# Half of the mask matmuls of the attention scores go: the second head of a pair is added onto the bank of the first, with the keys beside their negative

## The reference

```python
q = X @ Wq.T + bq                      # 32 heads of 16
k = encoder_output @ Wk.T + bk         # 8 groups of 16
v = encoder_output @ Wv.T + bv
scores = einsum('bgrqd,bgkd->bgrqk', q, k) / sqrt(16)
scores = where(causal_mask[None, None, None, :, :], -inf, scores)
scores = where(padding_mask[:, None, None, None, :], -inf, scores)
w = softmax(scores, axis=-1)
out = einsum('bgrqk,bgkd->bgrqd', w, v)
```

## Time and profile before

| | |
|---|---|
| time, median of 3 runs | 1948.77 us (1947.23 to 1953.24) |
| the profiled execution | 1954.19 us, span 1952.4 us |
| busy in the span | TensorE 86%, VectorE 55%, POOL 42%, ScalarE 38% |
| phase A | to about 625 us of the span |
| mean granted TensorE clock | 0.95 of full |

### The profile page before, as it was taken

One profiled execution on the slowest core, in us unless ns is written; L12 is line 12 of the kernel. 1 busy time (PEld: TensorE's weight loads), 2 busy tenths in 40 slices (PEclk: granted clock), 3 DMA queues, 4 the chain that ended last, 5 costly groups with the idle time before them and its releaser, 6 DMA issues. The chain is left out here.

```text
span 1952.4 us, 28974 instructions
## 1 busy us (share of the span) xinstructions
PE 1677.2 (86%) x10458; PEld 864.4 (44%) x10458; DVE 1077.9 (55%) x2244; ACT 736.4 (38%) x1326; POOL 828.0 (42%) x853
## 2 busy tenths in 40 slices
PE   5798888887875588888699996999999999888897
PEld 3455545444442243443266563444444444333343
DVE  6678777768663677776155664237755333211126
ACT  2468667666665454444122321221111111122221
POOL 1668656656455344444234532523534342011134
PEclk8999999999987799999799998999999999999999
DMA  5622123123022344443335442734654554366645
GB/s 144 157 66 80 47 55 82 44 55 77 17 68 63 59 97 101 93 93 77 60 69 130 97 87 56 161 88 104 146 112 105 114 124 98 71 151 155 153 132 181
DMA packets 423499, 188.82 MB, mean 97 GB/s; under 512 B 364792, under 2 KB 387576, under 8 KB 423360
## 3 DMA queue, kind: packets, MB, share of 16 engines
q1 hardware_dynamic: 417680, 168.36, 37.9%
q0 software_dynamic: 5680, 18.62, 3.4%
HBM read 77.82 MB, written 22.81 MB: 52 GB/s over the span
## 5 line engine op out<-in xcount | busy, mean ns | idle before, releaser
L894 POOL TENSOR_TENSOR a_pl<-a_prob,a_ph 128x512 f16<-128x512 f32 x256 | 298.5, 1180 | 206.1 <-ACT a_prob L810 204.7
L137 PE MATMUL bank<-XTh,d_whs 128*128 128x512 f16 x512 | 194.7, 380 | 0.9 <-ACT e_y L2256 0.7
L139 PE MATMUL bank<-XTh,d_wls 128*128 128x512 f16 x512 | 194.5, 380 | 0.0
L138 PE MATMUL bank<-XTl,d_whs 128*128 128x512 f16 x512 | 194.5, 380 | 0.0
L809 ACT ACTIVATE a_ph<-bank 128x512 f16<-128x512 f32 x256 | 154.3, 603 | 100.7 <-PE bank L612 77.0
L992 DVE TENSOR_REDUCE a_mx<-bank 128x2 f32<-128x512 f32 x256 | 165.7, 684 | 32.9 <-PE bank L598 29.7
L2094 POOL CAST d_cut<-d_raw 128x512 f16<-128x512 f32 x90 | 58.0, 645 | 234.3 <-DMA d_raw<-in_L_ffn_sw 152.7
L810 ACT ACTIVATE a_prob<-bank 128x512 f32<-128x512 f32 x256 | 155.2, 606 | 0.0
L2014 DVE TENSOR_TENSOR d_hid<-d_hid,bank 128x512 f32<-128x512 f32 x64 | 43.9, 686 | 181.6 <-PE bank L139 179.7
L610 PE MATMUL bank<-a_maddT,ident 128*128 128x512 f16 x256 | 103.4, 404 | 30.1 <-ACT a_prob L810 28.2
L1227 PE MATMUL bank<-b_wfc,b_xTh 128*128 128x512 f16 x256 | 99.5, 389 | 32.3 <-DMA b_xTl<-f_cut 25.9
(11 more groups left out here) (325 smaller groups left out, 4081.5 us busy)
## 6 DMA issues: line engine op xcount, KB each, us to landing
d_raw<-in_L_ffn_w SPq DMA_DIRECT2D x48, 256.0 KB, 3.0
d_raw<-in_L_ffn_sw SPq DMA_DIRECT2D x42, 256.0 KB, 3.1
made<-e_y SPq DMA_DIRECT2D x39, 256.0 KB
a_stage<-in_L_ffn_w_fc SPq DMA_DIRECT2D x32, 256.0 KB, 2.8
a_stage<-in_L_ffn_w_proj SPq DMA_DIRECT2D x32, 256.0 KB, 3.1
a_fbuf<-in_ctx SPq DMA_DIRECT2D x16, 256.0 KB, 3.7
rows<-f_cut SPq DMA_DIRECT2D x16, 256.0 KB, 2.4
out_x<-X SPq DMA_DIRECT2D x16, 256.0 KB
```

Of the source, the lines that this page charges most:

```text
L137: nc.tensor.matmul(out_ap, lhi, rhi, start=first, stop=False)
L138: nc.tensor.matmul(out_ap, lhi, rlo, start=False, stop=False)
L139: return nc.tensor.matmul(out_ap, llo, rhi, start=False, stop=last_one)
L894: nc.gpsimd.tensor_tensor(pl[:, n % NP, :], prob[:, n % 2, :], ph[:, n % NP, :], ALU.subtract).then_inc(ev["L"], 1)
```

## The change

A group in `ks` gets three slots: negated keys `kn`, keys `kp`, and zero. The pair (kp, 0) serves the first half and the pair (kn, kp) the second. The first half's matmul adds the upper head's scores to the mask, as before. The second half's matmul goes into the same bank without a new mask, after the first was read: it takes the upper head's scores (with its padding and maximum) away and adds the lower head's. The mask matmul is issued for `half == 0` alone. In the second pass n and n + 2 are the two halves and share a bank already; in the first pass the new `which` orders m so that m and m + 2 do. ScalarE's second copy of the high part is scaled by -1; VectorE makes the low parts of `kp` and `kn` in two subtractions of 128 x 128 where there was one of 128 x 256; `pad` holds the padding with both signs.

```diff
-    ks = sb("a_ks", [P, 2, G0, 4, STK], F16)
-    kd = ks[:, :, :, 0:4:3, :]
+    ks = sb("a_ks", [P, 2, G0, 3, STK], F16)
+    kn, kp = ks[:, :, :, 0, :], ks[:, :, :, 1, :]
...
+    def which(m):
+
+        u = m % 16
+        return m // 16, 2 * (u // 4) + u % 2, u // 2 % 2
...
# turn_k
-                        c = ks[:, tt, 4 * h + j // 2, 2 * (j % 2):2 * (j % 2) + 2, :].rearrange("p d c -> p (d c)")
+                        c = ks[:, tt, 4 * h + j // 2, 1 - j % 2:3 - j % 2, :].rearrange("p d c -> p (d c)")
...
# scores, and the same for tt, g, half in maxima
-                tt, g, half = m // 16, m // 2 % G0, m % 2
+                tt, g, half = which(m)
...
-                nc.tensor.matmul(bk[:, :].rearrange("p (r k) -> p r k", r=2), ident16[:, :],
-                                 madd[:, tt, :].unsqueeze(1).broadcast_to([P, 2, S]), start=True, stop=False)
+                if half == 0:
+                    nc.tensor.matmul(bk[:, :].rearrange("p (r k) -> p r k", r=2), ident16[:, :],
+                                     madd[:, tt, :].unsqueeze(1).broadcast_to([P, 2, S]), start=True, stop=True)
                 for r in range(2):
                     last = nc.tensor.matmul(bk[:, r * S:(r + 1) * S], qT[:, par, 2 * g + r, tt * P:(tt + 1) * P],
-                                            kT[:, par, 2 * g + half, :], start=False, stop=(r == 1))
+                                            kT[:, par, 2 * g + half, :], start=False, stop=True,
+                                            skip_group_check=True)
...
# turned_scores
-                nc.tensor.matmul(bk[:, :].rearrange("p (r k) -> p r k", r=2), ident16[:, :],
-                                 maddT[:, kc, :].unsqueeze(1).broadcast_to([P, 2, S]), start=True, stop=False)
+                if half == 0:
+                    nc.tensor.matmul(bk[:, :].rearrange("p (r k) -> p r k", r=2), ident16[:, :],
+                                     maddT[:, kc, :].unsqueeze(1).broadcast_to([P, 2, S]), start=True, stop=True)
...
# high_kv (ScalarE)
-                nc.scalar.activation(kd[:, tt, :, :, 0:HD0], k4, ACT.Copy)
-                nc.scalar.activation(kd[:, tt, :, :, 2 * HD0:3 * HD0], k4, ACT.Copy).then_inc(ev[f"hk{tt}"], 1)
+                nc.scalar.activation(p4, k4, ACT.Copy)
+                nc.scalar.activation(n4, k4, ACT.Copy, scale=-1.0).then_inc(ev[f"hk{tt}"], 1)
...
# low_kv (VectorE)
-                nc.vector.tensor_tensor(kd[:, tt, :, :, HD0:2 * HD0], k4, kd[:, tt, :, :, 0:HD0],
+                k3 = k32[:, tt, :].rearrange("p (g c) -> p g c", g=G0)
+                nc.vector.tensor_tensor(kn[:, tt, :, HD0:2 * HD0], kp[:, tt, :, 0:HD0], k3, ALU.subtract)
+                nc.vector.tensor_tensor(kp[:, tt, :, HD0:2 * HD0], k3, kp[:, tt, :, 0:HD0],
                                         ALU.subtract).then_inc(ev[f"lk{tt}"], 1)
```

More of the change, by code:

```diff
@@ L344, in phase_a @@
     maddT = sb("a_maddT", [P, 2, S], F16)
-    pad = sb("a_pad", [P, 2, B])
+    pad = sb("a_pad", [P, 2, B, 2])
     q32 = sb("a_q32", [P, D])
@@ L609, in turned_scores @@
                 wait("E", b, n + 1, NS)
-                nc.tensor.matmul(bk[:, :].rearrange("p (r k) -> p r k", r=2), ident16[:, :],
-                                 maddT[:, kc, :].unsqueeze(1).broadcast_to([P, 2, S]), start=True, stop=False)
+                if half == 0:
+                    nc.tensor.matmul(bk[:, :].rearrange("p (r k) -> p r k", r=2), ident16[:, :],
+                                     maddT[:, kc, :].unsqueeze(1).broadcast_to([P, 2, S]), start=True, stop=True)
                 nc.tensor.matmul(bk[:, :], kT[:, par, 2 * g + half, kc * P:(kc + 1) * P],
                                  qT[:, par, 2 * g:2 * g + 2, :].rearrange("p r q -> p (r q)"),
-                                 start=False, stop=True).then_inc(ev["ST"], 1)
+                                 start=False, stop=True, skip_group_check=True).then_inc(ev["ST"], 1)
             def times_v(b, par, n):
@@ L747, in high_kv @@
                 k4 = k32[:, tt, :].rearrange("p (g c) -> p g c", g=G0).unsqueeze(2).broadcast_to([P, G0, 2, HD0])
+                p4, n4 = (t[:, tt, :, 0:3 * HD0].rearrange("p g (r c) -> p g r c", r=3)[:, :, 0:3:2, :] for t in (kp, kn))
                 nc.scalar.activation(vv[:, par, tt, :, 0:HD0], v32[:, tt, :].rearrange("p (g c) -> p g c", g=G0),
                                      ACT.Copy).then_inc(ev[f"hv{tt}"], 1)
-                nc.scalar.activation(kd[:, tt, :, :, 0:HD0], k4, ACT.Copy)
-                nc.scalar.activation(kd[:, tt, :, :, 2 * HD0:3 * HD0], k4, ACT.Copy).then_inc(ev[f"hk{tt}"], 1)
+                nc.scalar.activation(p4, k4, ACT.Copy)
+                nc.scalar.activation(n4, k4, ACT.Copy, scale=-1.0).then_inc(ev[f"hk{tt}"], 1)
             def take_second(b, par, tt):
@@ L960, in bias_kv @@
                 wait(f"KV{tt}", b)
-                nc.vector.tensor_copy(kd[:, tt, :, :, ONE],
-                                      pad[:, tt, b:b + 1].unsqueeze(1).broadcast_to([P, G0, 2]))
+                nc.vector.tensor_copy(ks[:, tt, :, 0:2, ONE], pad[:, tt, b:b + 1, :].broadcast_to([P, G0, 2]))
                 nc.vector.tensor_tensor(v32[:, tt, :], bank[BM + 1][:, KV:2 * KV], bkv[:, KV:2 * KV], ALU.add)
@@ L974, in low_kv @@
                 wait(f"hk{tt}", b)
-                k4 = k32[:, tt, :].rearrange("p (g c) -> p g c", g=G0).unsqueeze(2).broadcast_to([P, G0, 2, HD0])
-                nc.vector.tensor_tensor(kd[:, tt, :, :, HD0:2 * HD0], k4, kd[:, tt, :, :, 0:HD0],
+                k3 = k32[:, tt, :].rearrange("p (g c) -> p g c", g=G0)
+                nc.vector.tensor_tensor(kn[:, tt, :, HD0:2 * HD0], kp[:, tt, :, 0:HD0], k3, ALU.subtract)
+                nc.vector.tensor_tensor(kp[:, tt, :, HD0:2 * HD0], k3, kp[:, tt, :, 0:HD0],
                                         ALU.subtract).then_inc(ev[f"lk{tt}"], 1)
@@ L1018, in _ @@
             nc.vector.memset(qs[:, :, :, ONE:ONE + 1], 1.0)
-            nc.vector.memset(kd[:, :, :, :, NEG:NEG + 1], 1.0)
+            nc.vector.memset(kp[:, :, :, NEG:NEG + 1], 1.0)
+            nc.vector.memset(kn[:, :, :, NEG:NEG + 1], -1.0)
             nc.vector.memset(vv[:, :, :, :, HD0:HD0 + 1], 1.0)
@@ L1039, in _ @@
             dve.wait_ge(k_tr, 1)
-            klink(nc.vector.tensor_copy(pad[:, :, :], bank[0][:, 0:2 * B].rearrange("p (t b) -> p t b", t=2)))
+            nc.vector.tensor_scalar(pad[:, :, :, 0], bank[0][:, 0:2 * B].rearrange("p (t b) -> p t b", t=2), -1.0, None,
+                                    ALU.mult)
+            klink(nc.vector.tensor_copy(pad[:, :, :, 1], bank[0][:, 0:2 * B].rearrange("p (t b) -> p t b", t=2)))
             dve.wait_ge(k_tr, 2)
```

## The result

The change makes the kernel slower: 1964.75 us median of five executions (1961.9 to 1968.88), where the kernel before took 1951.83 in five of its own, a ratio of 1.0064 with a 95% interval of [1.0046, 1.0082]. The forecast was 1936.7 us. The time lies above the range of 1923 to 1954 us, and the kernel became slower where faster was forecast.

The account below looks back on a forecast made before the run. TensorE and VectorE were taken as almost equally full in the scoring parts, with VectorE the bound beyond its waits. Gains of 12.6, 1.3 and 4.5 us less 6.3 of cost made -12.1: 1936.7 us, range 1923 to 1954.

Parts of the forecast that it names:

- the extra subtraction: First part of a round: VectorE's added 128x128 subtraction, blocked by POOL a third of the time, costs 6.3 us over 14.
- slower through the port: Rival, 8%: each added subtraction waits for POOL and pushes the next past another, 2.16 us each; 1961 us.
- Prelude: Element 0's scores, taken between 38 and 65 us with nothing else running: fewer masks shorten the bank loops, 1.3 us gained.
- Scoring parts: n = 15 to 30 of rounds 0 to 6: 2.4 us gained in each of four rounds, 1.0 in three, 12.6 together.
- short waits: VectorE's waits of 0.2 to 0.4 us for TensorE in scoring parts, 2.5 us in round 3, said to go nearly whole.
- the case that cancels: Rival, 24%: ScalarE's waits hold the scoring part's second half, only 6 us come back there, subtraction costs 9.8; 1947 us.
- last sign of being wrong: The forecast is wrong above all if scoring parts stay at 27 us because ScalarE's chain, not the maxima, paces them.
- First part: n = 0 to 14 of a round: turned scores lose masks, 0.65 us gained a round, 4.5 us for seven.
- The clock: Rival, 5%: with less to do in the scoring parts TensorE could be granted 1.2 GHz there, up to 2026 us.
- 0.215 us a matmul and not 0.4: Each mask matmul costs TensorE 0.215 us by starts; the rows' overlapping durations, near 0.4, would give 102 us.
- VectorE's 23 us in a scoring part: Round 3's scoring part: VectorE is busy 23.0 of 27.3 us and keeps that work after the change.
- The last round's masks: The last round, without first scores, is bound by ScalarE and POOL, so its 16 masks are worth nothing.

Follow-up runs that it names:

- e1: The changed kernel with all mask matmuls kept, so the change's extra work without its gain: 1966.08 us, ratio 1.0075 to the kernel before.
- e2: The changed kernel with one 128x256 subtraction in place of its two of 128x128 (one low part has the wrong sign): 1950.65 us, ratio 1.0000 to the kernel before.
- e10: e1 with the added subtraction made a one-input reduction of as many elements, into a slot nobody reads: 1951.71 us, ratio 1.0002 to the kernel before.
- e7: The whole change, with the negated low part of the keys made by ScalarE instead of VectorE: 1948.27 us, ratio 0.9985 to the kernel before.
- e12: e7 with the transposes of the activations placed after the round's weight loads on SyncE: 1944.92 us, ratio 0.9973 to the kernel before.
- e13: The kernel before, all masks kept, with the weight loads ahead of the transposes of the activations: 1951.55 us, ratio 1.0015 to the kernel before.
- The fills: Runs with added matmuls that nobody reads, placed where TensorE waits, among them e11, e16 and e15: ratios 0.9947 to 1.0066 to the kernel before.
- e11: e7 with matmuls that nobody reads at two places between the rounds: 1947.95 us, ratio 0.9991 to the kernel before.
- e16: The changed kernel with matmuls that nobody reads at two places between the rounds: 1964.01 us, ratio 1.0066 to the kernel before.
- e15: e12 with the matmuls between rounds that nobody reads, as in e11: 1939.28 us, ratio 0.9947 to the kernel before.
- e17: The changed kernel with the subtraction of the values' low part moved later, where TensorE's transposes don't wait for it: 1950.57 us, ratio 0.9997 to the kernel before.

## Why the prediction was wrong

**Two steps of the sum failed, the cost and the gain.** The sum was 18.4 us of gains against 6.3 of cost, -12.1; measured is +0.64%, some +13. The cost was about 15 us, and the gains, by the changed kernel against e1, about 2 (0.1%, not told from nothing). So 16 of the 25 us between forecast and result are gains that did not come, and 9 are cost.

**The cost: "the extra subtraction".** I took 0.45 us for each of 14, 6.3 us; e1 measures 0.75%, some 15 us, 1.05 us each, and e2 and e10 show that it is the second operation with two SBUF inputs. I asked how often the added operation would be blocked, and had that nearly right: 7 of 16, forecast five, and the keys' subtractions together took 0.40 to 0.44 us more in each call. I then let the operation behind it stay as it was: the values' subtraction took 0.47 to 0.75 us more in each call, and that is the term that I put at nothing. POOL issues its subtractions back to back, and VectorE gets one two-input operation through at each gap, or two: with two in a row the second often slipped in behind the first (median 0.28 us); with three the third did not. The case was written down as a rival, "slower through the port", at 2.16 us each and 8%; it was the right mechanism at half the size. With 1.05 us it would by my own sum not have been slower than before: 18.4 us of gains stood against it.

**The gain.** *Prelude*: 3.4 us in the pair of profiles (four profiles with all masks have 68.2 to 69.8 us there, the others 65.9 to 68.3), 1.3 forecast; of it nothing was kept, since part A of round 0 grew by 5.0 us, 2.3 to 2.9 of them in e2 and e7 as well, which have no extra subtraction. POOL waits there 4.2 us for the context's load, where it waited 2.0 in the kernel before, and the granted clock of that part is 0.74 where it was 0.94. How much of the growth is the earlier start, turned into waiting, is argued, not shown.

*Scoring parts*: 12.6 us forecast, 5.1 in B's sum. Rounds 0 to 3, 9.6 us by the forecast, gave nothing: 27.1, 26.8, 27.3 and 28.4 us against 26.9, 26.9, 27.9 and 27.3. The sentence that failed is that the short waits "go nearly whole". Many went (34 waits of VectorE for L604 over the rounds in place of 54, 21.5 us in place of 28.1), but the part is held in its middle by ScalarE's wait for a load, which I had named for the case that cancels and not for the forecast; what is gained ahead of it is waited away. It is the last sign of being wrong that the prediction names: the parts stay at 27 us because ScalarE's chain paces them. e12 shows it: without that chain rounds 0 to 3 take 26.1 us each with the masks halved, VectorE's waits for L604 are 15.2 us, the prediction's 15, and B differs by 12.7 us from e13's, with masks whole. Rounds 4 to 6, which have no such wait, gave 6.0 us where I had 3.0.

*First part*: the 4.5 us were not found. e2's A is 204.6 us and e7's 203.8, against 204.4 before. Rounds 1 to 6 of e7 are 3.2 us shorter than in the profile of the kernel before (154.1 against 157.3), but with all masks e13 has 153.2 there and e10 152.4.

*Between the rounds*: the sum had no term for C, and C grew by 10.8 us, by 7.1 to 10.0 in e2 and e7, more than B gained. In their profiles this takes back what their B, 5 us shorter, had gained; its cause is told under the clock.

**The clock.** The rival was right in what it saw: the mean granted clock of stage A fell from 0.94 to 0.88, and part of TensorE's work stood at 1.2 GHz. It was wrong in where. Not the scoring parts (1.00 in round 1, 0.94 in round 3), but the stretches around TensorE's waits: round 1's stretch between rounds in the changed kernel and in the kernel before,

```profile
196.90:213.40 16.50, 13.17 (x94) 7.30 (x92) 8.54 (x19) 5.12 (x10) 3.27 (x3) 0.79 0.17 49
```

```profile
192.60:206.80 14.20, 10.73 (x95) 6.25 (x94) 7.98 (x20) 4.63 (x8) 2.78 (x3) 1.00 0.19 57
```

is 2.3 us longer at 0.79. The fills take most of C's growth away although they add work, so the clock is its cause. Whether it costs the kernel time is open: e11 and e16 are no faster, e15 is, by as much as the theory said but within the intervals. The Trainium skill ("TensorE: Matmul & The Clock Gate", What's actually happening) lets the clock follow TensorE's recent activity; the fills agree, 0.88 to 0.94.

**What held.** 0.215 us a matmul and not 0.4: even the best case found, 8 us or 13 with the fill, is far below the 102 that busy times give. VectorE's 23 us in a scoring part stayed its work (23.9 in e12's 26.1). The last round's masks were worth nothing (21.3 us, 21.15 before). L976 and L979 as nearest rows were the right ones to look at.

## What to carry to other kernels

Before adding an operation of two SBUF inputs to VectorE, look at what POOL runs beside it and at the whole run of such operations behind the new one: the price can fall on the last of them. Here it disappeared when one of them moved off the path (e17) or to another engine (e7), and a reduction with one input in its place cost nothing (e10). When a shorter stage is expected to gain in every round, look first for one wait in its middle that has nothing to do with the change (here a load behind transposes); it takes back what is gained ahead of it. And the value of a removed matmul is its start-to-start time only where TensorE is what ends the waits; here half of 512 mask matmuls were worth 0 to 8 us, and 13 together with the fill, depending on what else stood on the path.

## What the runs showed of the hardware

A VectorE reduction with one SBUF input took 0.285 to 0.288 us in 16 of 16 cases beside a busy POOL; a subtraction of two SBUF inputs with as many elements took 0.28 or up to 1.24. A single small copy (L961 before, 128x16) had a median of 1.15 us; that this is the same effect was not tried. And with 256 matmuls less, TensorE's mean granted clock in stage A was 0.88 where it had been 0.94, and 0.88 and 0.89 in e2 and e7, which have no extra two-input operation on the path; matmuls that nobody reads brought it back.
